# Layer 1's scores from two fp32r products over 32 rows a head, instead of one fp32 product over 64 masked rows

## The reference

```
q = (x @ Wq.T).reshape(B, T, H, D).transpose(0, 2, 1, 3)     # H = 16, D = 16
k = (context @ Wk.T).reshape(B, S, H, D).transpose(0, 2, 1, 3)
q = rms_norm(q, q_norm_w);  k = rms_norm(k, k_norm_w)
q = apply_rope(q, q_cos, q_sin);  k = apply_rope(k, k_cos, k_sin)
attn = jnp.einsum('bhtd,bhsd->bhts', q, k) * scale           # scale = 16 ** -0.5
attn = jax.nn.softmax(attn, axis=-1)
```

## Time and profile before

| | |
|---|---|
| median of 3 runs | 2382.2 us |
| profiled execution, its own time | 2380.98 us |
| its span from first to last instruction | 2379.2 us |
| mean granted TensorE clock | 0.989 of 2.4 GHz |
| TensorE matmuls, busy | 2294.8 us (96%), 20320 records |
| VectorE, ScalarE, GpSimd busy | 1663.5, 1510.5, 1628.8 us (70%, 63%, 68%) |

### The profile page before, as it was taken

How to read it: one execution, slowest core, us unless ns; L and a number is a source line. 1 busy time by engine, 2 the same in 40 slices (tenths; PEclk the granted TensorE clock), 3 DMA queues, 4 the chain that set the end, 5 groups by cost and what they waited for, 6 DMA issues and landing times.

```text
span 2379.2 us, 61055 instructions
## 1 busy us (share of the span) xinstructions
PE 2294.8 (96%) x20320; PEld 1774.9 (75%) x20320; DVE 1663.5 (70%) x4061; ACT 1510.5 (63%) x4306; POOL 1628.8 (68%) x1830
## 2 busy tenths in 40 slices
PE   6999999999999999999999999999999999999578
PEld 5777777777787777777777777787777777777336
DVE  6766666776767667766666776767667666666785
ACT  4666666666666666666666666666666666666356
POOL 3676776676768767676776676767767676776507
PEclk9999999999999999999999999999999999999689
DMA  4000000000000000000000000000000000001202
GB/s 146 10 11 10 10 8 10 2 10 10 10 10 8 10 2 10 10 10 10 10 8 9 3 10 10 10 10 8 10 2 10 10 10 10 10 2 38 54 10 63
DMA packets 31197, 37.04 MB, mean 16 GB/s; under 512 B 3284, under 2 KB 29636, under 8 KB 31172
## 3 DMA queue, kind: packets, MB, share of 16 engines
q1 hardware_dynamic: 31172, 36.71, 5.3%
HBM read 29.36 MB, written 7.34 MB: 15 GB/s over the span
## 4 chain that ended last, share of the span: by engine, by line
PE 92%; DVE 3%; POOL 2%; issue 2%; ACT 1%; DMA 0%; POOLq 0%; SPq 0%; ACTq 0%; DVEq 0%
PE ps L349 25%; PE ps L410 17%; PE pt L434 11%; PE pa L446 7%; PE pt L424 5%; PE ps L393 5%; PE pa L486 4%; PE pa L461 4%; PE pa L349 2%; PE pt L349 2%; PE pa L584 1%; PE pt L609 1%; PE ps L474 1%; DVE th L1412 1%; PE pa L624 1%
## 5 line engine op out<-in xcount | busy, mean ns | idle before, releaser
L1048 DVE TENSOR_REDUCE nmx<-ps 112x2 f32<-112x750 f32 x512 | 480.1, 938 | 197.0 <-PE ps L410 190.9
L1508 POOL TENSOR_TENSOR prob<-prob,rinv 112x375 f32<-112x375 f32 x512 | 404.9, 812 | 197.6 <-DVE rinv L1056 197.6
L1508 POOL TENSOR_TENSOR f1w_room<-f1w_room,rinv 112x375 f32<-112x375 f32 x512 | 405.4, 817 | 64.3 <-DVE rinv L1056 64.3
L768 ACT ACTIVATE room<-ps 128x375 f32<-128x375 f32 (+2 forms) x480 | 227.8, 488 | 303.9 <-PE ps L349 303.9
L768 ACT ACTIVATE probT<-pt 125x336 f32<-125x336 f32 (+1 forms) x512 | 242.6, 474 | 195.8 <-PE pt L424 142.1
L808 ACT ACTIVATE prob<-ps,nmx 112x375 f32<-112x375 f32 x512 | 289.8, 580 | 65.7 <-DVE nmx L1048 65.7
L808 ACT ACTIVATE f1w_room<-ps,nmx 112x375 f32<-112x375 f32 x512 | 291.2, 587 | 2.4 <-DVE nmx L1048 2.3
L1533 POOL TENSOR_TENSOR krs<-krs,nhalf 125x48 f32<-125x48 f32 x32 | 256.9, 8030 | 0.0
L410 PE MATMUL ps<-kT,q 64*112 64x375 f32 x1024 | 234.6, 517 | 1.0 <-ACT prob L808 1.0
L410 PE MATMUL ps<-room,q 64*112 64x375 f32 x1024 | 230.7, 515 | 3.0 <-ACT prob L808 1.9
L1039 DVE COPY probT<-pt 125x336 f32<-125x336 f32 x322 | 162.7, 505 | 96.2 <-PE pt L434 96.2
(11 more groups left out here) (270 smaller groups left out, 5326.0 us busy)
## 6 DMA issues: line engine op xcount, KB each, us to landing
craw<-in_ctx SPq DMA_DIRECT2D x32, 375.0 KB, 3.1
xin<-in_x SPq DMA_DIRECT2D x32, 112.0 KB, 2.0
x_rows<-x SPq DMA_DIRECT2D x32, 112.0 KB, 1.9
out<-probT SPq DMA_DIRECT2D x16, 224.0 KB, 2.3
room<-x_rows SPq DMA_DIRECT2D x1, 2576.0 KB, 12.8
w<-in_f1w SPq DMA_DIRECT2D x2, 1024.0 KB, 6.7
stage<-in_wk SPq DMA_DIRECT2D x1, 1024.0 KB, 7.3
stage<-in_wv SPq DMA_DIRECT2D x1, 1024.0 KB, 9.8
```

Of the source, the lines that this page charges most:

```text
L768: return act.activation(dst, src, ACT.Copy)
L1048: top = dve.tensor_reduce(nmx[:, g:g + 2], ps[0:T, 2 * (i % 2):2 * (i % 2) + 2, 0:S], AX_X, ALU.max, negate=True)
L1508: pool.tensor_tensor(prob(i, n), prob(i, n), rinv[:, g:g + 1].to_broadcast([T, S]), ALU.mult).then_inc(s["normed"], 1)
```

## The change

The scale 1/4 goes into the query's norm (mean squares are no longer divided by 16) and the mask goes away. A head's keys are split into an upper part (`k1x[..., 0, :]`, written by ScalarE) and the rest (`k1x[..., 1, :]`, written by GpSimd); the two stand side by side, so that after the transposition they fill 32 rows of `kx`. Queries are split too, by VectorE: `q1x[:, 0]` is the upper part, `q1x[:, 1]` the rest, each written twice side by side. A head's scores are two fp32r matmuls over 32 rows, upper part and rest of the query against the same 32 rows of keys, added in PSUM. Transpositions are fp32r products with an identity `identr`. Four heads now make a tile, so there are four tiles of keys and two more of queries; the last two tiles of keys are turned after the first scores of layer 0. The tiles `kx` and `q1x` lie in the room of the FFN's `z`, `th` and `hr`.

```diff
-    HEADS1 = [8 * c + n for c in range(DC) for n in (0, 4, 2, 6, 1, 5, 3, 7)]
+    HEADS1 = [8 * c + n for c in range(DC) for n in (0, 2, 4, 6, 1, 3, 5, 7)]
...
+        k1x = sb("k1x", [SK, KT, H, 2, DH1], F32R)
+        qx = sb("qx", [P, 2, HT, T], F32R)
+        kx = sb("kx", [P, HT, SE], F32R)
+        q1x = sb("q1x", [T, 2, H, 2, DH1], F32R)
...
@@ TensorE, scores @@
-                        q, k = q1[r:r + 64, h // 8, h % 4, :], kT1[r:r + 64, h // 8, :]
-                    last = pe.matmul(ps[0:T, 2 * (i % 2) + n, 0:S], q, k, start=True, stop=True)
+                    for x in range(2):
+                        for n in range(2):
+                            h = HEADS1[2 * p + n]
+                            r = 32 * (h % 4)
+                            last = pe.matmul(ps[0:T, 2 * (i % 2) + n, 0:SE], qx[r:r + 32, x, h // 4, :],
+                                             kx[r:r + 32, h // 4, :], start=(x == 0), stop=(x == 1))
...
@@ TensorE, query_turn @@
-                pe.transpose(pa[:, 1, c * T:(c + 1) * T], q1b[:, c * P:(c + 1) * P], ident[0:T, 0:T])\
-                    .then_inc(s["q1T_ready"], 1)
+                if c == 1:
+                    pe.wait_ge(s["q1_sb"], b + 1)
+                for x in range(2):
+                    for g in range(2):
+                        heads = q1x[:, x, 8 * c + 4 * g:8 * c + 4 * g + 4, :, :].rearrange("p h y e -> p (h y e)")
+                        last = pe.matmul(pa[:, 1, (2 * x + g) * T:(2 * x + g + 1) * T], heads, identr[0:T, 0:T],
+                                         start=True, stop=True)
+                last.then_inc(s["q1T_ready"], 1)
+            def keys_turn(b, tiles):
+                for g in tiles:
+                    for t in range(KT):
+                        last = pe.matmul(pa[:, g % 2, t * (SK + 1):(t + 1) * (SK + 1)],
+                                         k1x[:, t, 4 * g:4 * g + 4, :, :].rearrange("p h x e -> p (h x e)"),
+                                         identr[0:SK, 0:SK + 1], start=True, stop=True)
+                    last.then_inc(s["k1T_ready"], 1)
...
@@ TensorE, rest @@
                 pe.wait_ge(s["k1_rope"], b + 1)
-                for c in range(DC):
-                    for t in range(KT):
-                        last = pe.transpose(pa[:, c, t * SK:(t + 1) * SK], k1b[:, t, c * P:(c + 1) * P],
-                                            ident[0:SK, 0:SK])
-                    last.then_inc(s["k1T_ready"], 1)
+                keys_turn(b, range(2))
...
                     scores(0, MIDDLE, b)
+                pe.wait_ge(s["k1T_sb"], b * HT + 2)
+                keys_turn(b, range(2, HT))
+                if not last_batch:
                     v0_proj(b + 1, [3])
...
@@ ScalarE, query_copies and rest @@
-                for m in range(4):
-                    ins = act.activation(q1[:, 1, m, :], pa[:, 1, T:2 * T], ACT.Copy, scale=mask1[:, m:m + 1])
-                ins.then_inc(s["q1_sb_act"], 1)
+                copy(qx[:, :, 2:4, :], pa[:, 1, 0:4 * T].rearrange("p (x g t) -> p x g t", x=2, g=2))\
+                    .then_inc(s["q1_sb_act"], 1)
...
+                act.wait_ge(s["k1_norm"], b + 1)
+                copy(k1x[:, :, :, 0, :], k1b.rearrange("p k (h e) -> p k h e", e=DH1)).then_inc(s["k1_hi"], 1)
                 act.wait_ge(s["am_ready"], b + 1)
...
-                for c in range(DC):
-                    act.wait_ge(s["k1T_ready"], b * DC + (c + 1))
-                    copy(kT1[:, c, :], pa[:, c, 0:S]).then_inc(s["k1T_sb"], 1)
+                for g in range(HT):
+                    act.wait_ge(s["k1T_ready"], b * HT + (g + 1))
+                    copy(kx[:, g, 0:S].rearrange("p (k s) -> p k s", k=KT),
+                         pa[:, g % 2, 0:KT * (SK + 1)].rearrange("p (k s) -> p k s", k=KT)[:, :, 0:SK]).then_inc(s["k1T_sb"], 1)
...
@@ VectorE, query_masks and query_scale @@
-                dve.tensor_tensor(q1[:, 0, :, :], pa[:, 1, 0:T].unsqueeze(1).to_broadcast([P, 4, T]),
-                                  mask1[:].unsqueeze(2).to_broadcast([P, 4, T]), ALU.mult).then_inc(s["q1_sb"], 1)
+                dve.tensor_copy(qx[:, :, 0:2, :], pa[:, 1, 0:4 * T].rearrange("p (x g t) -> p x g t", x=2, g=2))\
+                    .then_inc(s["q1_sb"], 1)
...
-                dve.tensor_tensor(half, half, qrs[:, 2, 8 * c:8 * c + 8].unsqueeze(2).to_broadcast([T, 8, DH1]),
-                                  ALU.mult).then_inc(s["q1_norm"], 1)
+                hi, lo = (q1x[:, x, 8 * c:8 * c + 8, :, :] for x in range(2))
+                twice = half.unsqueeze(2).to_broadcast([T, 8, 2, DH1])
+                link(dve.tensor_tensor(half, half, qrs[:, 2, 8 * c:8 * c + 8].unsqueeze(2).to_broadcast([T, 8, DH1]),
+                                       ALU.mult))
+                link(dve.tensor_copy(hi, twice))
+                dve.tensor_tensor(lo, twice, hi.bitcast(F32), ALU.subtract).then_inc(s["q1_norm"], 1)
...
@@ GpSimd, rest @@
                 pool.tensor_tensor(keys, keys, krs[:, 2, :].unsqueeze(2).to_broadcast([SK, KT * H, DH1]), ALU.mult)\
-                    .then_inc(s["k1_rope"], 1)
+                    .then_inc(s["k1_norm"], 1)
                 if not last_batch:
                     pool.wait_ge(s["x1_ready"], b + 1)
                     add_bias(b + 1)
+                pool.wait_ge(s["k1_hi"], b + 1)
+                by_head = k1x.rearrange("p k h x e -> p (k h) x e")
+                pool.tensor_tensor(by_head[:, :, 1, :], keys, by_head[:, :, 0, :].bitcast(F32), ALU.subtract)\
+                    .then_inc(s["k1_rope"], 1)
...
                 inverse_root(2, b)
+                pool.memset(kx[:, :, S:SE].bitcast(F32), 0.0).then_inc(s["k1_pad"], 1)
```

More of the change, by code:

```diff
@@ L22 @@
 U8_EPS = 1e-8
-DVE_STEPS = 21
+DVE_STEPS = 25
 POOL_STEPS = 7
@@ L139, in xattn_ffn_kernel @@
         k0_size, v0_size, k1_size = IC * SE, KT * INNER, KT * D
-        room = sb("room", [P, k0_size + v0_size + 3 * k1_size])
+        with nc.sbuf_tensor("room", [P, k0_size + v0_size + 3 * k1_size], F32) as room:
+            pass
+        kv0_room = sb("kv0_room", [P, k0_size + v0_size])
+        k1x = sb("k1x", [SK, KT, H, 2, DH1], F32R)
+        k1b_room = sb("k1b_room", [P, k1_size])
         kT0 = room[:, 0:k0_size].rearrange("p (c s) -> p c s", c=IC)
@@ L146, in xattn_ffn_kernel @@
         EARLY = min((k0_size + v0_size) // D, B - CH - 1)
-        q0_room = sb("q0", [P, 2 * IC * T])
-        q0 = q0_room[:, 0:IC * T].rearrange("p (j t) -> p j t", j=IC)
+        with nc.sbuf_tensor("q0_room", [P, 2 * IC * T], F32) as q0_room:
+            pass
+        q0 = sb("q0", [P, IC, T])
+        qx = sb("qx", [P, 2, HT, T], F32R)
         xn0T = sb("xn0T", [P, DC, T])
@@ L180, in xattn_ffn_kernel @@
         hp = sb("hp", [P, FC, T + 2])
-        z = sb("z", [P, FC, T])
-        th = sb("th", [P, FC, T])
-        hr = sb("hr", [T, F])
+        with nc.sbuf_tensor("z", [P, FC, T], F32) as z, nc.sbuf_tensor("th", [P, FC, T], F32) as th:
+            pass
+        kx = sb("kx", [P, HT, SE], F32R)
+        gate_back = sb("gate_back", [P, 2 * FC * T - HT * SE])
+        with nc.sbuf_tensor("hr", [T, F], F32) as hr:
+            pass
+        q1x = sb("q1x", [T, 2, H, 2, DH1], F32R)
         hq = sb("hq", [T, F], BF16)
@@ L401, in scores @@
                     pe.wait_ge(s["exped"], at(i - 1, part, b))
-                for n in range(2):
-                    if layer == 0:
+                if layer == 0:
+                    for n in range(2):
                         r = DH0 * n
[L405 to L408, removed]
-                        q, k = q1[r:r + 64, h // 8, h % 4, :], kT1[r:r + 64, h // 8, :]
-                    last = pe.matmul(ps[0:T, 2 * (i % 2) + n, 0:S], q, k, start=True, stop=True)
+                        last = pe.matmul(ps[0:T, 2 * (i % 2) + n, 0:S], q0[r:r + DH0, p, :], kT0[r:r + DH0, p, 0:S],
+                                         start=True, stop=True)
+                else:
+                    for x in range(2):
+                        for n in range(2):
+                            h = HEADS1[2 * p + n]
+                            r = 32 * (h % 4)
+                            last = pe.matmul(ps[0:T, 2 * (i % 2) + n, 0:SE], qx[r:r + 32, x, h // 4, :],
+                                             kx[r:r + 32, h // 4, :], start=(x == 0), stop=(x == 1))
                 last.then_inc(s["scores"], 1)
@@ L1637 @@
         "ident": np.eye(P, dtype=f),
-        "mask1": ((rows[:, None] // DH1 % 4 == np.arange(4)) * f(DH1 ** -0.5)).astype(f),
     }
```

23 lines of the change are left out of this document (12 added, 11 removed), and 2 rows, old and new, of the table names.

## The result

The changed kernel takes 2874.4 us (median of 4 runs, 2872.0 to 2883.13), the kernel before 2382.0 beside it: a ratio of 1.207 (95% interval 1.205 to 1.210). The forecast was slower, 2467, with a range to 2525. The direction was right, but the growth is 492 us where 85 was forecast: most of it was not in the sum at all.

What follows compares the result with a forecast made beforehand. TensorE was taken as the bound (96% busy, 92% of the chain). Keys 0.65, wait 0.2, queries 1.9 and scores -0.1 make 2.65 us a round, 82 over 31 rounds, plus 3 in the last batch: 2467 us, range 2415 to 2525.

Steps and rivals of the forecast that it cites:

- the paragraph on the queries: Start of attention: VectorE's uncovered copy and subtraction plus longer query turns delay TensorE by +1.9 us a round (+1.3 to +2.4).
- The rivals: Slow narrow products (chance 0.18), quarters one after another (0.10), a smaller loss (0.10), a faster kernel (0.08).
- Scores: Layer 1: only an even pair's scores are on the path, 0.69 instead of 0.72 us; -0.1 a round.
- the 0.22 for quarters to halves: Layer 1: assumed cost in us of changing the array's row split between new scores and the turning by rows.
- Keys: Key transposes: twelve matmuls instead of six, the second six on TensorE's path, +0.65 us a round.
- the rival of the slow narrow products: Key and query turns: narrow fp32r products go at fp32's pace, 1.65 us a round more, 2518 us; chance 0.18.
- The wait before the keys: First six key products wait for ScalarE's copy and GpSimd's subtraction: +0.2 us a round, bounds 0 and +0.6.
- ScalarE's part: ScalarE's new key copy starts L891 0.4 us later while VectorE quantises the other half; cost 0, at most +0.4.
- the places that were named: Where the round's growth should show: the key products, idle time before them, and the query stretch.
- The rival "faster": TensorE's count alone decides and VectorE's new work is covered: -0.7 us a round, 2359 us; chance 0.08.

Runs made afterwards that it cites:

- e4: The changed kernel with TensorE's idle gaps at the queries filled by 128-row bf16 matmuls whose results nobody reads: 2500.2 us.
- e3: The changed kernel with each score product taken over 64 rows instead of 32, two heads' numbers added, gaps kept: 2742.8 us.
- e13: The changed kernel, queries split behind their turn, gaps filled; GpSimd makes the keys' rest only after VectorE quantised both halves of layer 0's hidden rows: 2452.2 us.
- e14: The changed kernel, queries split behind their turn, gaps filled; GpSimd's subtraction of the keys in six pieces of 128 numbers instead of one: 2445.1 us.
- e1: The kernel before with only VectorE's added query copy and subtraction, written to unused room; old scores, keys and turns: 2441.2 us.

## Why the prediction was wrong, step by step

**The step that failed** is the one that closed the paragraph on the queries: "Behind it VectorE and ScalarE have idle time again, so nothing is given back, and nothing more is lost." All durations in the sum were taken at full clock. The gaps that the prediction itself counted, together with the new scores, brought the clock to 1.2 GHz behind them. It cost 374 us of the 492: the difference between the changed kernel (2874.4) and e4 (2500.2), which has the same work and more. e4 is 118 above the kernel before, where 85 was forecast. The rivals had no mechanism for the clock either. In the kernel before the clock is full all through the loop (2.4 GHz from 100 to 2206 us) and its mean of 0.989 comes from what stands behind it, so nothing in the rows warned of this. The direction would have come out right without the clock too, as e4 shows, but that of the 492 us is the smaller part. The Trainium skill, "TensorE: Matmul & The Clock Gate", Part 1, says that the low clock is the default and that activity releases it. The runs agree that the clock went with what TensorE did, and add that a busy TensorE isn't enough (27.16 of 27.30 us at half clock). Which property of the new scores counts stays open, as said of e3.

**The sum at full clock.** e4's rounds take 72.26, so 3.62 more than before; 2.65 was forecast. The rows that the prediction read as two pairs of layer 1 begin with scores of layer 0 (`ps<-room,q`). The couple with layer 1's scores is the one before it, and takes the same 3.82, from here to 1080.30:

```profile
1076.48 0.89 PE L410 MATMUL ps<-kT,q 64*112 64x375 f32 x4
```

- *Scores: -0.03 a couple forecast, -0.18 measured.* Even scores to turning take 0.53 (117.92 to 118.45), not 0.69: of the 0.22 for quarters to halves 0.06 is left. The turning by rows then takes 0.81 (118.45 to 119.26), where it took 0.60, so the switch costs 0.2 on the way back to quarters. The odd scores are hidden behind ScalarE's copy, as forecast, with 0.18 of idle time to spare. The quarters do run side by side: four products of 376 columns in 0.53.
- *Keys: +0.65 forecast, 0.72 measured,* the second group from 1270.76 to 1271.48:

```profile
1268.27 0.86 PE L517 MATMUL pa<-identr,k1x 125*128 125x126 f32 x6
1268.97 1.04 PE L632 MATMUL pt<-f0w_q,hqT 128*112 128x256 bf16 x8
...
1270.76 0.88 PE L517 MATMUL pa<-identr,k1x 125*128 125x126 f32 x6
1271.48 0.68 PE L357 MATMUL ps<-wv_hi,cT_lo 128*125 128x512 f32 x2
```

  Both groups take 0.12 a product, near the 0.11 of the sum and far from the 0.20 of the rival of the slow narrow products, which falls.
- *The wait before the keys: +0.2 forecast; 0.61 measured, and elsewhere,* ahead of the hidden rows' turn:

```profile
1267.75 0.70 PE L622 MATMUL pt<-identb,hq 112*128 112x112 bf16 x8 [0.61 <-DVE hq L1282]
```

  GpSimd's subtraction took 1.82 (1.74 forecast) and was in time for the keys. What was missed is that it held up VectorE. The price "0, at most +0.4" for ScalarE's part looked at the wrong engine.
- *Queries: +1.9 forecast, about 2.5 measured* (from the first turn's place to the values behind pair 2's turning). TensorE's timeline of the first round, still at full clock:

```profile
103.69 0.66 PE L509 MATMUL pa<-identr,q1x 112*128 112x112 f32 x4 [0.51 <-DVE q1x L1107]
...
106.87 0.17 PE L430 MATMUL pt<-identb 64*128 64x1 bf16 x1 [0.34 <-DVE probT L1068]
...
108.45 0.55 PE L445 MATMUL pt<-ident,f1w_room 112*125 112x112 f32 x3 [0.19 <-ACT probT L795]
109.97 0.55 PE L445 MATMUL pt<-ident,f1w_room 112*125 112x112 f32 x3 [0.96 <-DVE probT L1064]
...
110.85 2.50 PE L457 MATMUL pa<-probT,room 125*64 125x112 f32 x24
```

  The first turn waited 0.51 and came 0.67 late against its neighbour before it (0.8 forecast). A turn of four products took 0.58 instead of 0.19: +0.4 each, not 0.33. The wait inside pair 2's turning is 0.96, where 1 was forecast, but the half before it comes late as well. The reason for that is below: VectorE's second `query_scale`, timeline of the kernel after:

```profile
106.55 0.72 DVE L1104 TENSOR_TENSOR q1b<-q1b,qrs 112x128 f32<-112x128 f32 x1
107.30 0.78 DVE L1106 CAST q1x<-q1b 112x256 fp32r<-112x256 f32 x1
108.12 0.43 DVE L1107 TENSOR_TENSOR q1x<-q1b,q1x 112x256 fp32r<-112x256 f32 x1
```

The first `query_scale` of that round took 0.29, 0.29 and 0.42. Here GpSimd's two products with the reciprocals run at the same time, from 106.31. That these two are the same effect as L1282's was not tried by itself. The Trainium skill, "SBUF — State Buffer", section Who interferes with whom, says that VectorE with two SBUF inputs, or in a fast two-port mode, and a GpSimd instruction that reads SBUF share a pair of ports, and that the one that starts first keeps it for its whole length. e13 and e14 agree for L1282. That rule spoke against this change and was not weighed.

In the round these terms make -0.54 (three couples), 0.72, 0.61 and 2.5, so 3.3 of the 3.62; the last 0.3 was not traced to a row. Of the places that were named, only the wait lies elsewhere. Against the forecast the largest miss at full clock is the queries' 0.6. The rival "faster" needed VectorE's work to be covered; e1, which has that work and nothing else, costs 59.5 us, so it was not.

## What to carry to other kernels

Before an edit that makes matmuls shorter or narrower, or leaves TensorE waiting, ask what the granted clock will be, and price the stretch behind the edit at half clock too: here gaps of 1.45 us a round cost 1.9 with the old scores around them (e1, 59.5 us over 31 to 32 rounds), and with the new scores and gaps of 2.00 the clock took 12 more (374 us). An idle gap of TensorE that can't be closed may be worth filling with wide matmuls that nobody reads. And a SBUF operation given to GpSimd is also a price on VectorE's fast or two-input operations that fall beside it.

## What was not expected of the hardware

- Filling TensorE's gaps in each round with 34 bf16 matmuls of 128 rows took a kernel from 2874 to 2500 us; the same with 32 rows left it at 2848 to 2904.
- The clock stayed low through layer 1's pairs although TensorE was busy for 27.16 of 27.30 us, and rose only behind the first scores of layer 0.
- A VectorE operation of 0.43 us takes 1.77 beside a GpSimd operation of 1.82.
- Six GpSimd operations of 128 numbers take 2.94 us, with VectorE at work beside two of them, where one of 768 takes 1.83.
